# Graph attention and product-key attention: a fourth set of rows fetched one by one, and a reordered start

## The chip, the cores and the metric

The kernel runs on one core of one Trainium2 chip. The metric is the device time of one execution in microseconds (us); before the change it is 10136.64 us, the median of 3 runs (10135.63 to 10138.01).

## The reference

Input: `x` of 8 batches of 1024 tokens of 128 numbers, an adjacency matrix of 1024 x 1024, small weights, and two tables of 131072 rows of 128 numbers (keys and values). Two blocks are added to `x` in turn:

```
x = x + elu(softmax(leaky(e_src + e_dst), masked by adj) @ Wh)      # h = layernorm(x), Wh = h @ W
h = layernorm(x)
q = (h @ Wq) * 128**-0.5                                            # 8 heads of 128
for each of 2 halves: scores against 128 keys, the 16 best          # product keys
of the 16*16 sums the 16 best -> softmax weights kv_scores, table rows ind
k = sum of 16 weighted rows of keys_table[ind];  v = the same of values_table[ind]
out = causal softmax(q k^T) @ v, 1024 x 1024 in each head and batch
x = x + out @ Wo
```

So for each batch, head and token 16 rows of a table must be fetched whose numbers are known only at run time: 8 x 8 x 1024 x 16 rows. Keys and values stand side by side in one table here, so a row is 256 numbers, 1 KB.

## The kernel before

The work is cut into 64 heads (8 batches of 8 heads; n counts them from 0) of 8 units of 128 tokens; (n, t) is unit t of head n. All engines run programs written out by hand and meet only at semaphores.

**VectorE (DVE)** in step t of head n: it chooses the 16 rows of unit (n+1, t) (`choose_sets`, `choose_sums`, `choose_rows`) and, between these, adds up the rows of unit (n, t) that were fetched a head earlier (`add_row`, `sum_rows`, L920 and L931). `choose_rows` leaves the row numbers in `idx` (`idx_ready`, L1006), `sum_rows` frees the buffers (`rows_summed`, L931). So the row numbers of a unit are known about 8 steps before its sum.

**GpSimd (POOL)** fetches: `gathers(t)` (L346) issues one indirect DMA for each of the 16 places of a unit's list, and each brings 128 rows, one for every token, into `ring`, which has room for 4 units. Before unit t of head n it waits for `idx_ready` of that unit and for `rows_summed` of the unit four earlier.

**Single transfers.** For the units in `SETS`, the 16th place is not fetched by POOL but row by row, 128 transfers of 1 KB, into `far`. SyncE (SP) does the sets `FAR = (3, 7)`: `far_begin` copies the 128 addresses into one row of memory (L278), `far_fetch` loads them into registers 32 at a time and issues one transfer each (L293). ScalarE (ACT) does the set of unit 0 (`NEAR`): `near_begin` in step 1 (L468), and `near_fetch` at the end of steps 1 to 7 with 20, 20, 20, 20, 16, 16 and 16 rows (L483). A set may be fetched again only after `rows_summed` of its unit in the head before. Head 0 uses none: POOL issues 128 gathers for it and 125 for each of the 63 others.

**TensorE (PE)** adds the first 8 of 16 rows of a unit as products with diagonal matrices (`weigh`, L656), which ACT makes (`diagonals`, L437), and does all attention products; ACT does the exponentials (`attend_exp`, L446) and copies.

**SP's order.** In each head the sets in turn; at a batch's start `load(b + 2)` (waits until the graph part of the batch before is done, `g_xn`), and in `turn` the eight stores of the finished batch between the two sets.

**The start.** SP issues x, weights, the whole adjacency (4 MB), then the key tensors. PE and ACT make `wh` (own terms, L595), then `dst` (L599), then four groups of key products (L733), then exp, transposes and sum of graph tile 0. DVE makes the mask of all 8 tiles, then the edges of tile 0 (`graph_edges`, L849 to L862). A loop over the 8 tiles of batch 0 follows: finish tile `it` (`graph_elu`, from L872, `graph_out`, `graph_norm`), edges of tile it+1, choose the rows of unit (0, it). From `it = 2` (`LEAD`) on it also sums unit it-2. So units 0 to 5 of head 0 are summed in this loop, and units 6 and 7 (`SUMMED` and the next) only in steps 6 and 7 of head 0.

Of the kernel before, what the change touches and what calls it, by code (L numbers as in the profile page):

```python
# [5 lines left out]
ALU = mybir.AluOpType  # L6
# [8 lines left out]
P = 128  # L15
BATCH = 8
# [16 lines left out]
FAR = (3, 7)  # L33
NEAR = 0
NEAR_ROWS = (0, 20, 20, 20, 20, 16, 16, 16)
SETS = FAR + (NEAR,)
FAR_ROW = TOPK - 1
# [9 lines left out]
def gat_and_product_key_attention(nc, x, adj, W, WT, a, WqpkT, keysT, Wq, table, Wo, out):  # L47
    with ExitStack() as ctx:
# [6 lines left out]
        def sem(name):  # L55
            return ctx.enter_context(nc.semaphore(name))
# [89 lines left out]
        in_dma = sem("in_dma")  # L146
        adj_dma = sem("adj_dma")
# [98 lines left out]
        def _(sp):  # L246
# [33 lines left out]
            def far_fetch(n, i):  # L280

                sp.wait_ge(far_row_dma[i], n * 16)
                sp.sem_inc(sp_mark, 1)
                if not (isinstance(n, int) and n == 1):
                    sp.wait_ge(rows_summed, (n - 1) * UNITS + SETS[i] + 1)
                    sp.sem_inc(sp_mark, 1)
                for q in range(0, P, LOADED):
                    _, at = nc.values_load_multi_w_load_instructions(
                        far_row[0:1, i, q:q + LOADED], engines=[mybir.EngineType.SP],
                        min_val=0, max_val=(HEADS * NUM_KV - 1) * KV_BYTES,  # L290
                        skip_runtime_bounds_check_because="made of two positions below 128 and a head below 8")
                    for j in range(LOADED):
                        sp.dma_start(far[q + j:q + j + 1, i, :].bitcast(U8), table_bytes[bass.ds(at[j], KV_BYTES)]) \  # L293
                            .then_inc(far_dma[i], 16)
# [11 lines left out]
            def turn(b):  # L306
                far_sets((b + 1) * HEADS, range(0, last_set))
                stores(b)
                far_sets((b + 1) * HEADS, range(last_set, last_set + 1))
# [3 lines left out]
            far_begin(1, 0)  # L313
            far_fetch(1, last_set + 1)
            with sp.Fori(1, HEADS) as h:
                far_sets(h, range(len(FAR)))
            with sp.Fori(0, BATCH - 2) as b:
                load(b + 2)
                turn(b)
                with sp.Fori(1, HEADS) as h:  # L320
                    far_sets((b + 1) * HEADS + h, range(len(FAR)))
            turn(BATCH - 2)
            with sp.Fori(1, HEADS - 1) as h:
                far_sets((BATCH - 1) * HEADS + h, range(len(FAR)))
            far_sets(BATCH * HEADS - 1, range(len(FAR)), True)
# [41 lines left out]
        def _(act):  # L367
            def projection(bn):
# [5 lines left out]
                for t in range(TILES):  # L374
                    act.wait_ge(wh_mm, TILES * bn + t + 1)
                    nc.scalar.copy(wh[:, t, :], ps_p[:, t % 2, 0:P + 1]).then_inc(wh_copied, 1)
                for c in range(2):
                    act.wait_ge(dst_mm, 2 * bn + c + 1)
                    nc.scalar.copy(dst[:, c * 512:(c + 1) * 512], ps_p[:, c, :]).then_inc(dst_copied, 1)

# [89 lines left out]
            def near_fetch(n, part):  # L470

                if NEAR_ROWS[part - 1] == 0:
                    act.wait_ge(far_row_dma[near], n * 16)
                    act.sem_inc(act_mark, 1)
                    act.wait_ge(rows_summed, (n - 1) * UNITS + NEAR + 1)
                    act.sem_inc(act_mark, 1)
                q = sum(NEAR_ROWS[:part])
                _, at = nc.values_load_multi_w_load_instructions(
                    far_row[0:1, near, q:q + NEAR_ROWS[part]], engines=[mybir.EngineType.Activation],
                    min_val=0, max_val=(HEADS * NUM_KV - 1) * KV_BYTES,  # L480
                    skip_runtime_bounds_check_because="made of two positions below 128 and a head below 8")
                for j in range(NEAR_ROWS[part]):
                    act.dma_start(far[q + j:q + j + 1, near, :].bitcast(U8), table_bytes[bass.ds(at[j], KV_BYTES)]) \  # L483
                        .then_inc(far_dma[near], 16)
# [4 lines left out]
            projection(0)  # L489

            for g in range(4):
                act.wait_ge(pk_mm, g + 1)
                nc.scalar.copy(pk[:].rearrange("p h s n -> p (h s n)")[:, g * 512:(g + 1) * 512],
                               ps_s[:, g % 2 * 512:(g % 2 + 1) * 512]).then_inc(pk_copied, 1)
            act.wait_ge(in_dma, 4 * 16)
# [19 lines left out]
            def head(b, h, n, graph, ahead, first=False):  # L515
                if ahead and not first:
                    query_weights((h + 1) % HEADS, n + 1)
                for t in range(UNITS):
# [21 lines left out]
                    if t < UNITS - 1:  # L540
                        if not first or t + 1 > SUMMED:
                            diagonals(n, t + 1)
                    elif ahead:
                        diagonals(n + 1, 0)
# [8 lines left out]
                    if ahead and t >= 1 and not first:  # L553
                        near_fetch(n + 1, t)
# [20 lines left out]
        def _(pe):  # L575
            def projection(bn):
# [14 lines left out]
                for t in range(TILES):  # L591

                    if t >= 2:
                        pe.wait_ge(wh_copied, TILES * bn + t - 1)
                    nc.tensor.matmul(ps_p[:, t % 2, 0:P + 1], hnT[:, t * P:(t + 1) * P], w_ext[:],  # L595
                                     start=True, stop=True).then_inc(wh_mm, 1)
                pe.wait_ge(wh_copied, TILES * (bn + 1))
                for c in range(2):
                    nc.tensor.matmul(ps_p[:, c, :], w_dst[:], hnT[:, c * 512:(c + 1) * 512],  # L599
                                     start=True, stop=True).then_inc(dst_mm, 1)  # L600

# [123 lines left out]
            projection(0)  # L725

            pe.wait_ge(in_dma, 4 * 16)
            for g in range(4):
                if g >= 2:
                    pe.wait_ge(pk_copied, g - 1)  # L730
                for j in range(4):
                    m = 4 * g + j
                    ins = nc.tensor.matmul(ps_s[:, (4 * (g % 2) + j) * P:(4 * (g % 2) + j + 1) * P],  # L733
                                           wpk_t[:, m, :], keys_t[:, m, :], start=True, stop=True)
                ins.then_inc(pk_mm, 1)
            pe.wait_ge(dst_copied, 2)
            graph_transposes(0)
            graph_sum(0, 0, ps_s)
# [12 lines left out]
            def head(b, h, n, graph, ahead, first=False):  # L751
# [52 lines left out]
        def _(dve):  # L804
# [217 lines left out]
            projection(0)  # L1022
            dve.wait_ge(adj_dma, 16)
            for t in range(TILES):
                c = step(nc.vector.tensor_scalar(mask[:, t, :], mask[:, t, :].bitcast(I32), 0, -BIG,
                                                 ALU.is_le, ALU.mult))
            after(c)
            graph_edges(0, 0, 0)
            for it in range(TILES):
                graph_elu(it, it, ps_s)  # L1030
# [12 lines left out]
                choose_rows(it, it, c)  # L1043
                weights(it, it)
# [18 lines left out]
            def head(b, h, n, graph, ahead, first=False):  # L1063
                for t in range(UNITS):
# [16 lines left out]
                    dve.wait_ge(dve_rows_dma[t], gathered(n, t))  # L1081
                    if first and t < SUMMED:
# [69 lines left out]
```

## Time and profile before

| | before |
|---|---|
| time, median of 3 runs | 10136.64 us |
| span of the profiled execution | 10159.7 us |
| POOL busy | 7625.7 us (75%), 8003 gathers |
| DVE busy | 6962.0 us (69%) |
| PE busy | 5615.2 us (55%) |
| ACT busy | 3117.0 us (31%) |
| single transfers of SP, of ACT | 16256, 7936 |

The profile gives one execution; its own time is known only as the span, which is 23.1 us over the median of the runs. Busy time leaves out the time that an engine takes to issue DMAs, so ACT's 31% holds none of its 7936 single transfers, and SP has no busy time at all. For POOL the gather itself counts, and the short stretch between two gathers is shown as "issue".

### The profile page before, as it was taken

The page shows a single profiled execution, that of the slowest core. Times are in us where ns is not written, and L with a number is a line of the kernel's source. Part 1 is how long each engine was busy: PE and PEld are TensorE (multiplying, and loading weights), DVE is VectorE, ACT ScalarE, POOL GpSimd, SP SyncE. Part 2 cuts the span into 40 slices and gives each one's busy share as a digit, 9 for nine tenths or more (in the row PEclk, how much of TensorE's full clock was granted, in tenths as well). Part 3 has the DMA queues.
Part 4 walks back from the last instruction along what each step waited for, and adds up shares of the span by engine and source line. Part 5 has one row for each costly group of instructions (what it writes and reads, how often), then busy time and mean ns, then how long its engine had stood idle before and what let it go on. Part 6 is the DMA issues. An engine that isn't in the chain of part 4 may idle for free.

```text
span 10159.7 us, 173542 instructions
## 1 busy us (share of the span) xinstructions
PE 5615.2 (55%) x23108; PEld 4511.4 (44%) x23108; DVE 6962.0 (69%) x42780; ACT 3117.0 (31%) x9770; POOL 7625.7 (75%) x8020
## 2 busy tenths in 40 slices
PE   5655555555555555555555555555555555555555
PEld 4544444444444444444444444444444444444444
DVE  8866667666666667666776666766667676666663
ACT  4333233332333333333333233333333333322222
POOL 5777777777777777777777777777777777777776
PEclk7777777777777777777777777777777777777777
DMA  3333333333333333333333333333333333333333
GB/s 109 104 108 108 108 112 108 108 108 108 112 108 107 108 108 112 108 108 108 108 112 108 108 108 108 112 108 108 107 110 110 108 108 108 108 110 108 108 108 99
DMA packets 481297, 1099.25 MB, mean 108 GB/s; under 512 B 180864, under 2 KB 222720, under 8 KB 479968
## 3 DMA queue, kind: packets, MB, share of 16 engines
q0 software_dynamic: 384144, 1049.48, 36.1%
q1 hardware_dynamic: 71152, 31.60, 1.2%
q10 hardware_dynamic: 24800, 8.19, 0.4%
q14 instruction: 1184, 9.70, 0.3%
q8 instruction: 17, 0.28, 0.0%
HBM read 1084.36 MB, written 4.19 MB: 107 GB/s over the span
## 4 chain that ended last, share of the span: by engine, by line
POOL 73%; issue 24%; DVE 2%; PE 1%; POOLq 0%; DMA 0%; ACT 0%; ACTq 0%; SPq 0%; DVEq 0%
POOL ring L346 73%; DVE hot L998 0%; PE ps_o L709 0%; DMA wo<-in_Wo 0%; DVE ps_v L920 0%; POOLq L362 0%; PE ps_p L595 0%; POOLq L360 0%; DMA ring<-in_table,idx 0%; PE ps_p L599 0%; ACTq L483 0%; PE ps_s L681 0%; DVE nmax L1049 0%; PE ps_w L656 0%; DVE edge L849 0%
## 5 line engine op out<-in xcount | busy, mean ns | idle before, releaser
L346 POOL DMA_INDIRECT ring<-in_table,idx x8003 | 7624.1, 953 | 2507.7 <-issue 2440.8
L656 PE MATMUL ps_w<-ring,diag 128*128 128x256 f32 x8192 | 1996.2, 400 | 9.7 <-DMA ring<-in_table,idx 9.6
L700 PE MATMUL ps_p<-ident,prob 128*128 128x128 f32 x2304 | 548.8, 390 | 2576.1 <-ACT prob L446 2568.1
L656 PEld LDWEIGHTS ps_w<-ring,diag 128*128 128x128 f32 x8192 | 1630.3, 205 | 244.8 <-issue 12.7
L917 DVE TENSOR_SCALAR ps_v<-ring,wgt 128x256 f32<-128x256 f32 x512 | 248.7, 486 | 2147.8 <-DMA ring<-in_table,idx 2147.8
L998 DVE SCALAR_TENSOR_TENSOR hot<-rank,posf,cand 128x54 f32<-128x54 f32 x8192 | 1655.4, 270 | 0.3
L700 PEld LDWEIGHTS ps_p<-ident,prob 128*128 128x128 f32 x2304 | 371.4, 194 | 2769.7 <-ACT prob L446 1734.0
L920 DVE SCALAR_TENSOR_TENSOR ps_v<-ring,wgt,ps_v 128x256 f32<-128x256 f32 x3072 | 1478.1, 481 | 19.6
L437 ACT ACTIVATE diag<-ident,wgt 128x128 f32<-128x128 f32 x4096 | 1251.9, 391 | 0.0
L668 PE MATMUL ps_t<-ident,kv 128*128 128x128 f32 x512 | 234.4, 458 | 1642.4 <-DVE kv L931 1642.4
L709 PEld LDWEIGHTS ps_o<-probT,kv 128*128 128x128 f32 x4608 | 1040.8, 318 | 145.9 <-ACT probT L454 69.9
L446 ACT ACTIVATE prob<-ps_s,nmax 128x128 f32<-128x128 f32 (+7 forms) x512 | 378.1, 738 | 2324.8 <-issue 1777.3
L709 PE MATMUL ps_o<-probT,kv 128*128 128x128 f32 x4608 | 1035.4, 404 | 43.7 <-ACT probT L454 43.7
L668 PEld LDWEIGHTS ps_t<-ident,kv 128*128 128x128 f32 x512 | 92.1, 180 | 1803.4 <-DVE kv L931 1802.7
L681 PE MATMUL ps_s<-kT,qT 128*128 128x512 f32 (+3 forms) x1536 | 784.6, 630 | 1.6 <-issue 1.2
L998 DVE DVE_READ_ACCUMULATOR hot<-rank,posf,cand 128x1 f32 x8192 | 651.3, 79 | 0.0
L634 PE MATMUL ps_v<-pk,xt 128*128 (+1 forms) x1026 | 545.6, 632 | 13.6 <-ACT xt L412 7.5
L931 DVE TENSOR_TENSOR kv<-part,ps_w 128x256 f32<-128x256 f32 x512 | 215.7, 421 | 453.9 <-PE ps_o L709 407.0
L454 ACT COPY probT<-ps_p 128x512 f32<-128x512 f32 (+3 forms) x768 | 351.7, 480 | 414.2 <-PE ps_p L700 412.3
L681 PEld LDWEIGHTS ps_s<-kT,qT 128*128 128x128 f32 x1536 | 366.7, 271 | 194.9 <-issue 188.2
L441 ACT COPY kT<-ps_t 128x128 f32<-128x128 f32 x512 | 135.9, 265 | 977.6 <-PE ps_t L668 977.4
L941 DVE MAX8 side<-ps_v 128x8 f32<-128x128 f32 x1024 | 253.6, 289 | 212.2 <-issue 181.0
(119 smaller groups left out, 8053.9 us busy)
## 6 DMA issues: line engine op xcount, KB each, us to landing
far<-in_table SPq DMA_DIRECT2D x16256, 1.0 KB
ring<-in_table,idx POOLq DMA_INDIRECT x8003
far<-in_table ACTq DMA_DIRECT2D x7936, 1.0 KB
xin<-in_x SPq DMA_DIRECT2D x8, 512.0 KB, 4.6
mask<-in_adj SPq DMA_DIRECT2D x1, 4096.0 KB, 14.6
out_x<-acc SPq DMA_DIRECT2D x64, 64.0 KB
far_row<-far_at SPq DMA_DIRECT2D x127, 0.5 KB
far_row<-far_at ACTq DMA_DIRECT2D x62, 0.5 KB
```

The costliest lines, as they stand in the source:

```text
L346: pool.indirect_dma_start(out=ring[:, t % RING, k, :], out_offset=None, in_=table, in_offset=bass.IndirectOffsetOnAxis(ap=idx[:, t, k:k + ...
L437: nc.scalar.mul(diag[:, k, :], ident[:], wgt[:, t, k:k + 1]).then_inc(diag_ready, 1)
L446: nc.scalar.activation(prob[:, 0:cols], ps_s[:, 0:cols], ACT.Exp, bias=nmax[:, 0:1], accum_out=psum_row[:, 0:1]).then_inc(p_exp, 1)
L454: nc.scalar.copy(probT[:, c * 512:c * 512 + m], ps_p[:, c, 0:m]).then_inc(p_copied, 1)
L634: nc.tensor.matmul(ps_sim, xt[:, t % 2, :], pk[:, bass.ds(h, 1), :, :].rearrange("p o s n -> p (o s n)"), start=True, stop=True).then_inc( ...
L656: ins = nc.tensor.matmul(pw_ps, diag[:, k, :], ring[:, t % RING, k, :], start=(k == 0), stop=(k == PE_ROWS - 1))
L668: nc.tensor.transpose(ps_t[:, 0, :], kv[:, t, 0:P], ident[:]).then_inc(k_tp, 1)
L681: nc.tensor.matmul(ps_s[:, c * 512:c * 512 + m], q, kT[:, c * 512:c * 512 + m], start=True, stop=(c < HALVES[t] - 1))
L700: ins = nc.tensor.transpose(ps_p[:, c, (j % 4) * P:(j % 4 + 1) * P], prob[:, j * P:(j + 1) * P], ident[:])
L709: ins = nc.tensor.matmul(oT_ps, kv[:, j, P:KV], probT[:, j * P:(j + 1) * P], start=(j == 0), stop=(j == t))
L920: row_sum[0] = step(nc.vector.scalar_tensor_tensor(out=part[:] if k == TOPK - 1 else ps_part, in0=rows, scalar=w, in1=ps_part, op0=ALU.mul ...
L998: c = step(nc.vector.scalar_tensor_tensor(out=hot[:, k, :], in0=rank[:], scalar=posf[:, k:k + 1], in1=cand[:, 1, :], op0=ALU.is_equal, op1 ...
```

## The change

- `FAR = (1, 3, 6)` instead of `(3, 7)`; with unit 0 there are four sets, so POOL has 124 gathers in each head from head 1 on.
- SP fetches rows 32 to 127 of unit 1's set and all rows of the sets of units 3 and 6: 352 in a head, 256 before.
- ACT fetches the set of unit 0 in steps 1 to 5 (28, 28, 24, 24, 24 rows) and rows 0 to 31 of unit 1's set in steps 6 and 7 (16 each), the latter in head 0 too: 160 in a head, 128 before.
- SP begins the next set (`far_begin`) before the last 32 rows of the one it is in, not before its first; the batch's stores move to the same place in the third set.
- Start: the adjacency's first tile is loaded ahead of the keys and the rest behind them; `dst` is made before the own terms; graph tile 0's exp, transposes and sum (now in `wh_ps`) move ahead of the last two groups of key products; the masks of tiles 1 to 7 move behind the edges of tile 0; the edges of tile 1 move behind the choice of unit (0, 0).
- Head 0: units 6 and 7 are weighed and summed in steps 1 and 2 (`LATE`), and in these two steps PE waits for the sum before the next similarities.

```diff
-FAR = (3, 7)
+LATE = {1: SUMMED, 2: SUMMED + 1}
+FAR = (1, 3, 6)
 NEAR = 0
-NEAR_ROWS = (0, 20, 20, 20, 20, 16, 16, 16)
+SHARED = 0
 SETS = FAR + (NEAR,)
+ACT_ROWS = (32, 0, 0, P)
+NEAR_PLAN = {1: ((3, 0, 28),), 2: ((3, 28, 56),), 3: ((3, 56, 80),), 4: ((3, 80, 104),), 5: ((3, 104, 128),),
+             6: ((0, 0, 16),), 7: ((0, 16, 32),)}
...
-            sp.dma_start(mask[:].bitcast(I32), adj.rearrange("(t p) n -> p t n", p=P)).then_inc(adj_dma, 16)
-            sp.dma_start(wpk_t, WqpkT).then_inc(in_dma, 16)
-            sp.dma_start(keys_t, keysT).then_inc(in_dma, 16)
+            sp.dma_start(mask[:, 0, :].bitcast(I32), adj[0:P, :]).then_inc(adj_first_dma, 16)
+            sp.dma_start(wpk_t, WqpkT).then_inc(pk_dma, 16)
+            sp.dma_start(keys_t, keysT).then_inc(pk_dma, 16)
+            sp.dma_start(mask[:, 1:TILES, :].bitcast(I32), adj[P:N, :].rearrange("(t p) n -> p t n", p=P)) \
+                .then_inc(adj_dma, 16)
...
-                for q in range(0, P, LOADED):
+                for q in range(first, P, LOADED):
+                    if q == P - LOADED:
+                        if follow is not None:
+                            far_begin(*follow)
+                        if after_begin is not None:
+                            stores(after_begin)
...
-            def far_sets(n, sets, final=False):
-                for i in sets:
+            def far_sets(n, final=False, stored=None):
+                for i in range(len(FAR)):
                     if i < last_set:
-                        far_begin(n, i + 1)
-                    elif not final:
-                        far_begin(n + 1, 0)
-                    far_fetch(n, i)
+                        far_fetch(n, i, ACT_ROWS[i], follow=(n, i + 1))
+                    else:
+                        far_fetch(n, i, ACT_ROWS[i], stored, None if final else (n + 1, 0))
...
             with sp.Fori(0, BATCH - 2) as b:
                 load(b + 2)
-                turn(b)
+                far_sets((b + 1) * HEADS, stored=b)
...
+            projection(0, True)
+            graph_exp(0)
+            keep_products(range(2))
+            graph_copy(0)
+            keep_products(range(2, 4))
+            act.wait_ge(in_dma, 2 * 16)
             nc.scalar.copy(wq_cur[:], wq[:, 0, :]).then_inc(wq_copied, 1)
-            graph_exp(0)
-            graph_copy(0)
...
-                    if ahead and t >= 1 and not first:
-                        near_fetch(n + 1, t)
+                    if ahead:
+                        for i, lo, hi in NEAR_PLAN.get(t, ()):
+                            if i == SHARED or not first:
+                                near_fetch(n + 1, i, lo, hi)
...
+            pe.wait_ge(pk_dma, 2 * 16)
+            key_products(range(2))
+            pe.wait_ge(wh_copied, TILES)
             graph_transposes(0)
-            graph_sum(0, 0, ps_s)
+            graph_sum(0, 0, wh_ps)
+            key_products(range(2, 4))
+            pe.wait_ge(in_dma, 2 * 16)
...
-                    if not first or t >= SUMMED:
+                    if not first:
                         weigh(n, t, graph)
+                    elif t in LATE:
+                        weigh(n, LATE[t], False)
...
+                        if first and t in LATE:
+                            pe.wait_ge(rows_summed, LATE[t] + 1)
                         similarities(n1 % HEADS, n1 * UNITS + t1, t1)
...
-                if it < TILES - 1:
+                if 0 < it < TILES - 1:
                     graph_edges(0, it + 1, it + 1)
                 c = choose_sets(0, it, it)
...
                 choose_rows(it, it, c)
+                if it == 0:
+                    graph_edges(0, 1, 1)
                 weights(it, it)
...
+                    u = LATE.get(t, t) if first else t
+                    dve.wait_ge(dve_rows_dma[u], gathered(n, u))
+                    if first and u != t:
+                        c = choose_sums(n, u, a_unit, c, add_row)
+                        sum_rows(n, u)
+                        choose_rows(t, a_unit, c)
```

## Rows read from the trace of the kernel before

**Rows 1.** The page, part 4: the chain that ended last, by engine
```profile
POOL 73%; issue 24%; DVE 2%; PE 1%; POOLq 0%; DMA 0%; ACT 0%; ACTq 0%; SPq 0%; DVEq 0%
```

**Rows 2.** Waits of POOL: us in total, times, longest us
```profile
POOL ring L346 <- DVE idx L1006: 55.8, 1, 55.8
POOL ring L346 <- DVE kv L931: 11.1, 4, 10.2
```

**Rows 3.** Windows, gathers alone: stretch, length, busy (count), clock, DMA share, GB/s
```profile
58.00:308.90 250.90, 183.09 (x190) 0.77 0.36 103
...
308.90:10135.00 9826.10, 7441.03 (x7813) 0.73 0.38 109
```

**Rows 4.** Timeline of POOL: start us, us, instruction, idle before and releaser
```profile
58.08 1.10 POOL L346 DMA_INDIRECT ring<-in_table,idx  x1 [55.80 <-DVE idx L1006]
...
78.52 1.14 POOL L346 DMA_INDIRECT ring<-in_table,idx  x1 [0.30 <-issue]
...
308.93 0.95 POOL L346 DMA_INDIRECT ring<-in_table,idx  x1 [0.30 <-issue]
...
10133.13 0.94 POOL L346 DMA_INDIRECT ring<-in_table,idx  x1 [0.30 <-issue]
```

**Rows 5.** Timeline of SP, one set in head 7
```profile
1262.81 0.49 SPq L278 DMA_DIRECT2D far_row<-far_at  x1
1265.76 48.38 SPq L293 DMA_DIRECT2D far<-in_table  x128
```

**Rows 6.** Waits of SP, whole span
```profile
SPq L276 <- DVE idx L1006: 3170.9, 126, 32.4
```

**Rows 7.** Timeline of ACT, one part of the set of unit 0
```profile
1110.71 6.65 ACTq L483 DMA_DIRECT2D far<-in_table  x20
```

**Rows 8.** Waits of DVE, 1100 to 1257 us, one head
```profile
DVE ps_v L917 <- DMA ring<-in_table,idx: 37.1, 7, 7.8
```

**Rows 9.** Timeline of DVE and POOL: sum of unit (16, 0), first gather of (16, 4)
```profile
2636.19 0.42 DVE L931 TENSOR_TENSOR kv<-part,ps_w 128x256 f32<-128x256 f32 x1 [8.99 <-PE ps_o L709]
...
2667.61 0.95 POOL L346 DMA_INDIRECT ring<-in_table,idx  x1 [0.30 <-issue]
```

**Rows 10.** Timeline of all engines, the start
```profile
12.77 4.70 PE L595 MATMUL ps_p<-w_ext,hnT 128*128 128x129 f32 x16 [0.68 <-ACT hnT L373]
...
17.82 3.78 PE L599 MATMUL ps_p<-hnT,w_dst 128*128 128x512 f32 x4 [0.36 <-ACT wh L376]
...
22.40 1.67 DVE L849 SCALAR_TENSOR_TENSOR edge<-dst,wh,mask 128x256 f32<-128x256 f32 x4
...
24.98 6.96 PE L733 MATMUL ps_s<-ring 64*128 64x128 f32 x32 [3.37 <-DMA wo<-in_Wo]
...
34.07 1.15 ACT L383 ACTIVATE hn<-edge,row 128x1024 f32<-128x1024 f32 x1
...
42.03 0.35 DVE L872 TENSOR_SCALAR hp<-ps_s,row 128x128 f32<-128x128 f32 x1 [6.52 <-PE ps_s L617]
...
42.67 0.31 ACT L393 ACTIVATE hneg<-hneg 128x128 f32<-128x128 f32 x1 [4.65 <-DVE hneg L874]
...
44.99 1.67 DVE L849 SCALAR_TENSOR_TENSOR edge<-dst,wh,mask 128x256 f32<-128x256 f32 x4
...
46.31 1.22 PE L634 MATMUL ps_v<-pk,xt 128*128 128x256 f32 x2 [0.85 <-ACT xt L412]
...
49.55 0.49 DVE L941 MAX8 side<-ps_v 128x8 f32<-128x128 f32 x2
...
57.63 0.17 DVE L1006 CAST idx<-idxf 128x16 uint32<-128x16 f32 x1
...
74.00 0.17 DVE L1006 CAST idx<-idxf 128x16 uint32<-128x16 f32 x1
```

**Rows 11.** Timeline of ACT and DVE, end of head 0 and sum of unit (1, 0)
```profile
291.07 1.11 ACT L446 ACTIVATE prob<-ps_s,nmax 128x1024 f32<-128x1024 f32 x1 [3.22 <-DVE nmax L1049]
...
296.45 0.42 DVE L931 TENSOR_TENSOR kv<-part,ps_w 128x256 f32<-128x256 f32 x1 [0.70 <-PE ps_o L709]
```

More of the change, by code:

```diff
@@ L367, in _, with own_terms, projection @@
         def _(act):
-            def projection(bn):
+            def own_terms(bn):
+                for t in range(TILES):
+                    act.wait_ge(wh_mm, TILES * bn + t + 1)
+                    nc.scalar.copy(wh[:, t, :], ps_p[:, t % 2, 0:P + 1]).then_inc(wh_copied, 1)
+            def projection(bn, dst_first=False):
                 act.wait_ge(hvar, bn + 1)
@@ L373, in projection @@
                     nc.scalar.copy(hnT[:, c * 512:(c + 1) * 512], ps_p[:, c, :]).then_inc(hnT_copied, 1)
-                for t in range(TILES):
-                    act.wait_ge(wh_mm, TILES * bn + t + 1)
-                    nc.scalar.copy(wh[:, t, :], ps_p[:, t % 2, 0:P + 1]).then_inc(wh_copied, 1)
+                if not dst_first:
+                    own_terms(bn)
                 for c in range(2):
@@ L488, in _, with keep_products @@
             nc.scalar.copy(w_dst[:], wh_ps[:, 1:P + 1]).then_inc(aux_copied, 1)
[L489 to L495, printed above, removed]
+            def keep_products(groups):
+                for g in groups:
+                    act.wait_ge(pk_mm, g + 1)
+                    nc.scalar.copy(pk[:].rearrange("p h s n -> p (h s n)")[:, g * 512:(g + 1) * 512],
+                                   ps_s[:, g % 2 * 512:(g % 2 + 1) * 512]).then_inc(pk_copied, 1)
+            projection(0, True)
[4 more added lines that the diff above has]
+            act.wait_ge(in_dma, 2 * 16)
             nc.scalar.copy(wq_cur[:], wq[:, 0, :]).then_inc(wq_copied, 1)
-            graph_exp(0)
-            graph_copy(0)
             for it in range(TILES):
@@ L539, in head @@
                     attend_begin(n, t)
[L540 to L543, printed above, removed]
+                    if first and t == 1:
+                        diagonals(n, SUMMED + 1)
+                    if not first and t < UNITS - 1:
+                        diagonals(n, t + 1)
+                    elif ahead and t == UNITS - 1:
                         diagonals(n + 1, 0)
@@ L575, in _, with own_terms, projection @@
         def _(pe):
-            def projection(bn):
+            def own_terms(bn):
+                for t in range(TILES):
+                    if t >= 2:
+                        pe.wait_ge(wh_copied, TILES * bn + t - 1)
+                    nc.tensor.matmul(ps_p[:, t % 2, 0:P + 1], hnT[:, t * P:(t + 1) * P], w_ext[:],
+                                     start=True, stop=True).then_inc(wh_mm, 1)
+            def projection(bn, dst_first=False):
                 if not isinstance(bn, int):
@@ L590, in projection @@
                     pe.wait_ge(aux_copied, 2)
[L591 to L597, printed above, removed]
+                if not dst_first:
+                    own_terms(bn)
+                    pe.wait_ge(wh_copied, TILES * (bn + 1))
                 for c in range(2):
@@ L724, in _, with key_products @@
             pe.wait_ge(consts, 5 + HEADS)
[L725 to L736, printed above, removed]
+            projection(0, True)
+            def key_products(groups):
+                for g in groups:
+                    if g >= 2:
+                        pe.wait_ge(pk_copied, g - 1)
+                    for j in range(4):
+                        m = 4 * g + j
+                        ins = nc.tensor.matmul(ps_s[:, (4 * (g % 2) + j) * P:(4 * (g % 2) + j + 1) * P],
+                                               wpk_t[:, m, :], keys_t[:, m, :], start=True, stop=True)
+                    ins.then_inc(pk_mm, 1)
+            pe.wait_ge(pk_dma, 2 * 16)
+            key_products(range(2))
+            pe.wait_ge(wh_copied, TILES)
             graph_transposes(0)
-            graph_sum(0, 0, ps_s)
+            graph_sum(0, 0, wh_ps)
+            key_products(range(2, 4))
+            pe.wait_ge(in_dma, 2 * 16)
             for it in range(TILES):
@@ L1022, in _, with masks @@
             projection(0)
-            dve.wait_ge(adj_dma, 16)
[L1024 to L1028, printed above, removed]
+            def masks(tiles):
+                for t in tiles:
+                    c = step(nc.vector.tensor_scalar(mask[:, t, :], mask[:, t, :].bitcast(I32), 0, -BIG,
+                                                     ALU.is_le, ALU.mult))
+                after(c)
+            dve.wait_ge(adj_first_dma, 16)
+            masks(range(1))
+            dve.wait_ge(wh_copied, 1)
+            graph_edges(0, 0, 0)
+            dve.wait_ge(adj_dma, 16)
+            masks(range(1, TILES))
+            dve.wait_ge(wh_copied, TILES)
             for it in range(TILES):
-                graph_elu(it, it, ps_s)
+                graph_elu(it, it, ps_s if it else wh_ps)
                 graph_out(0, it, it, True)
                 graph_norm(it)
-                if it < TILES - 1:
+                if 0 < it < TILES - 1:
                     graph_edges(0, it + 1, it + 1)
```

49 lines of the change are left out of this document (25 added, 24 removed).

## The prediction

> **What bounds the kernel now.** I read the page first and in it the chain of waits: POOL and the "issue" between its gathers make 97% of the chain that ended last [rows 1]. The waits of POOL say whether it is ever held up: 55.8 us before its first gather, and 11.1 us in 4 waits for a sum of DVE, 10.2 of them in one [rows 2]; going through all 8003 gathers in the timeline, that one, at 259 to 269 us, is the only place where a gather starts over 1.6 us after the one before. The busy shares mislead here: POOL is shown 75% busy and is never free. The windows give the pace. From the 191st gather at 308.93 to the end of the last, which starts at 10133.13, there are 7813 [rows 3, 4]; (10133.13 + 1.25 - 308.93) / 7813 = 1.2576 us each. So the time is the start of the first gather, 8003 gathers at 1.26 us, one wait, and a tail of 10159.7 - 10134.4 = 25.3 us after the last.
>
> The sum below is made against the profiled execution, whose span is 10159.7 us, 23.1 us (0.23%) over the median 10136.64. I take the saving off both alike.
>
> **One gather less in each of 63 heads.** Head 1 has 61 gathers in its first four units instead of 62, and 62 more are saved behind them. I count the 62 here: 62 x 1.2576 = 78.0 us. The one of head 1 comes up below. It is worth this only if the 128 rows are fetched beside POOL in time, so each cover is checked.
>
> **SP.** A set of 128 rows takes 48.38 us, 0.378 us a row, and 2.95 us pass from the copy of the addresses to the first row [rows 5]. 352 rows are 133.1 us; the three begins are issued inside the sets now, so their landing is mostly hidden: 4 us a head is my estimate, 9 the upper bound (three times 2.95). SP needs 137 to 142 us of a head of 124 x 1.2576 = 155.9 us. It fits with 14 to 19 us to spare; before it waited 3170.9 us for row numbers [rows 6], some 50 us a head. At each batch's start `load` now stands ahead of the set of unit 1 and waits for the graph's tile of step 5, which holds that set back by some 4 steps (80 us). The sets have about 8 steps (156 us) from row numbers to sum, and SP makes up 14 us or more in each head: cost nothing, at most a few us if a set is late. The stores stand behind a wait for the row numbers of step 1, by when DVE has added the last unit of the batch: nothing.
>
> **ACT.** 20 rows take 6.65 us, 0.333 us each [rows 7]; 32 more rows are 10.7 us a head: 8 more rows (2.7 us) in steps 1, 2 and 5, 4 more (1.3 us) in steps 3 and 4. Queued behind them is the next `attend_exp`, for which PE waits, then `turn_keys` and similarities, then DVE. So I let all of it fall on DVE's loop. The cover is that DVE stands idle 37.1 us of a head for rows of POOL [rows 8]; 26 us remain. POOL feels DVE's lateness only through the ring. It is tightest at the batches' starts, where PE and ACT make the projection: the sum of unit (16, 0) ends at 2636.6 and the gather that needs it starts at 2667.6, a margin of 31 us [rows 9]. A head's 10.7 us and the 1.3 us by which POOL comes earlier leave 19. Cost nothing; without the cover it would be up to 12 us in each of 6 batches. DVE's extra address column is one small instruction a head, under the same cover.
>
> **The start, up to the first gather.** `dst` takes from its first product to the edges 22.40 - 17.82 = 4.6 us; made first, it is ready at 12.77 + 4.6 = 17.4. The first own term adds 1, so the edges of tile 0 begin at 18.4 and, as the block takes 49.55 - 44.99 = 4.6, end at 23.0 [rows 10]. ACT has the own terms until 22.4, then loads the exp's table (1.3) and starts the exp at 23.7, against 34.07 [rows 10]. From that start to the tile's sum read by DVE it was 42.03 - 34.07 = 8.0; half the key products, 3.5 us of 6.96, keep PE until 25.7, which adds 0.7: 32.3. But ACT now has to copy the last two key groups, which PE makes from 32.3 to 35.8, before the tile's next exponential: that runs at 36.5, not at 33. From there to the end of the similarities it was 46.31 + 1.22 - 42.67 = 4.9: 41.4. Choosing takes 57.80 - 49.55 = 8.25: row numbers at 49.6, first gather at 49.9, 8.2 us earlier than 58.08.
>
> **The second unit takes that back.** POOL is through with unit (0, 0) 20.4 us later, at 70.3 [rows 4]. The edges of tile 1 now start only when unit 0 is chosen: 49.6 + 4.6 = 54.2, exp, transposes and sum 8.0: 62.2, and from there to row numbers 57.80 - 42.03 = 15.8: 78.0, against 74.17 before [rows 10]. So POOL starts unit (0, 1) at 78.3, against 78.52: it waits 8 us and has won 0.2. Bounds: 70.3 (no wait, 8.2 won) and 82 (3.5 lost). I take the worked-out value. DVE is 3.8 us late in the rest of the loop, and POOL, with the list 4.3 us ahead there before, still does not wait.
>
> **Head 0.** Summing units 6 and 7 in steps 1 and 2 takes away what POOL waited 10.2 us for. What is late next is the sum of unit (1, 0), which frees the ring for (1, 4). It ended at 296.9 [rows 11]. It comes later by the loop's 3.5 us (0.3 made good) and by ACT's 32 rows in steps 6 and 7, 10.7 us of which its idle time before the exponentials covers 3.2 [rows 11] and, I estimate, 1.5 in the step before: 6 us. The two sums only change places. That gives 306.4. POOL, held by nothing, would be there at 308.93 - 10.2 - 1.3 (head 1's gather less) - 0.2 = 297.2. It waits 9 us, and (1, 4) starts at 306.6: 2.3 us won. Bounds for this place: 297 less a few us if DVE runs earlier too (up to 12 won) and 316 (ACT's rows and PE's two new waits for the sum all on the path, 7 lost). Units (1, 5) to (2, 3) follow with margins of 3 to 10 us by the same reckoning; the tail stays.
>
> **Sum.** 78.0 + 2.3 = 80.3 us: span 10079.4, time 10136.6 - 80.3 = 10056.3, say 10056. Its own range is 10047 to 10066, from the bounds of the last paragraph.
>
> **Rivals.** (a) Both early gains last: unit (0, 1) does not wait and (1, 4) does not: 78.0 + 10.2 + 1.3 + 8.2 = 97.7, 10039. For it: the start is indeed shorter; against it: the dependence through the edges of tile 1. (b) POOL meets new waits later, at batches' starts or while DVE catches up in heads 1 to 3: 1 to 4 us in each of 7 places, 10060 to 10084. For it: ACT's rows fall where DVE catches up, and in head 1 SP has all its sets to do at once; against it: the 31 us margin. (c) Slower: SP becomes the bound. It decides from 352 r + 4 = 157.2 (the head before), r = 0.435 us a row; each 0.01 beyond costs 3.5 us a head, 222 us in all, so r = 0.45 gives about 10460. Against it: 0.378 was measured with ACT issuing at the same time. (d) The row-by-row transfers slow the gathers as much as they replace them, and nothing is won: 10137. Against it: the DMA engines are busy 38% of the time [rows 3], and POOL's pace is set by issuing, not by landing.
>
> The Trainium skill speaks for (d): in "DMA: Bandwidth & Descriptors", section "Issuing engines are not separate DMA queues", it says that DMAs started by different engines run on the same 16 DMA engines, and that spreading them saves only the sequencer's issue time. If the DMA engines were the bound, this change would bring nothing. Here the issue time is exactly what binds, so rule and forecast agree on this trace, and the rule would bite only with the DMA share near full.
>
> **How the numbers follow.** Forecast 66%, (a) 10%, (b) 18%, (c) 3%, (d) 3%. The range 10042 to 10074 holds the forecast, half of (a) and most of (b). It also takes in that the gathers' pace may move: 0.001 us each is 8 us in all, and DVE's work per gather rises by 0.8%. 0.2% is about what a measurement of this kernel can tell from none, 20 us. Faster by more than that are the forecast, (a) and (b): 0.94. Same 0.03 (d), slower 0.03 (c).
>
> **What would show it.** Right: 7940 gathers at 1.257 to 1.259 us; the first near 50, the second unit's first near 78 with a wait of about 8 us on row numbers; no wait near 259; one of several us for a sum near 297; none after 320; SP's sets at 48.4 us for 128 rows, with its wait for row numbers down to some 15 us a head. Wrong: waits of POOL in every head or batch, rows of SP above 0.40 us, a pace off 1.2576 by more than 0.002, or a first gather later than 58.

## The result, and the profile after

The changed kernel takes 10064.62 us (median of 4 runs, 10059.83 to 10070.11) beside 10137.33 us for the kernel before: ratio 0.9927, 95% interval 0.9915 to 0.9939. It saves 72.7 us; 80 were forecast.

| | before | after |
|---|---|---|
| time, median | 10137.33 us | 10064.62 us |
| span of the profiled execution | 10159.7 us | 10063.9 us |
| gathers | 8003 | 7940 |
| POOL, DVE, ACT busy | 7625.7, 6962.0, 3117.0 us | 7545.1, 6958.9, 3072.9 us |

The two spans differ by 95.8 us, the times by 72.7, because the profile of before comes from an execution 23 us slower than its median: its gathers follow each other at 1.2576 us, those of after at 1.2549 us, which over 7813 gathers makes 20.9 us that the change did not bring. Below, "pace" is this time from one gather's start to the next where POOL never waits.

Waits of POOL in the kernel after (us in total, times, longest) answer to [rows 2]; the waits are now one of idx before the first gather and one before the second unit, and a long one filed under "issue":

```profile
POOL ring L352 <- issue: 2438.8, 7933, 19.5
POOL ring L352 <- DVE idx L1040: 54.8, 6, 45.7
```

Timeline of POOL after, beside [rows 4]; start, duration, and in brackets the idle time before:

```profile
47.96 1.10 POOL L352 DMA_INDIRECT ring<-in_table,idx  x1 [45.68 <-DVE idx L1040]
...
67.10 0.97 POOL L352 DMA_INDIRECT ring<-in_table,idx  x1 [0.30 <-issue]
76.01 0.94 POOL L352 DMA_INDIRECT ring<-in_table,idx  x1 [7.95 <-DVE idx L1040]
...
292.86 0.95 POOL L352 DMA_INDIRECT ring<-in_table,idx  x1 [0.30 <-issue]
313.33 0.99 POOL L352 DMA_INDIRECT ring<-in_table,idx  x1 [19.52 <-issue]
...
10038.83 0.95 POOL L352 DMA_INDIRECT ring<-in_table,idx  x1 [0.30 <-issue]
```

The gather at 313.33 is the first of unit (1,4), the same place as 308.93 in [rows 4]. The profile names no releaser, but the sum it needs, of unit (1,0), ends just ahead of it. Timeline of DVE after, the sums of units (0,5), (1,0) and (2,0):

```profile
186.84 0.42 DVE L965 TENSOR_TENSOR kv<-part,ps_w 128x256 f32<-128x256 f32 x1
...
312.11 0.42 DVE L965 TENSOR_TENSOR kv<-part,ps_w 128x256 f32<-128x256 f32 x1 [8.27 <-PE ps_o L734]
...
456.32 0.42 DVE L965 TENSOR_TENSOR kv<-part,ps_w 128x256 f32<-128x256 f32 x1 [9.81 <-PE ps_o L734]
```

The windows view of the gathers from there on (columns as in [rows 3]):

```profile
313.20:10041.00 9727.80, 7362.62 (x7751) 0.74 0.39 110
```

Nothing waits in this stretch. So in the two traces: 62 gathers less, 77.8 us at 1.2549; (1,4) starts 4.4 us later; the tail is 1.5 us shorter; 20.9 us are pace. 77.8 - 4.4 + 1.5 = 74.9, against 72.7 by the times.

### The profile page after: what moved, and what is told of

Same layout as the page of the kernel before. It is cut to its first block, busy times and chain, and to the rows that moved or that the text cites. A ratio compares the mean times of both kernels' runs of the same rounds, so it can differ in the third digit from the quotient of the medians.

```text
span 10063.9 us, 190428 instructions
## 1 busy us (share of the span) xinstructions
PE 5503.5 (55%) x23108; PEld 4468.0 (44%) x23108; DVE 6958.9 (69%) x42844; ACT 3072.9 (31%) x9770; POOL 7545.1 (75%) x7957
## 4 chain that ended last, share of the span: by engine, by line
POOL 72%; issue 24%; DVE 2%; PE 1%; ACTq 1%; POOLq 0%; ACT 0%; DMA 0%; SPq 0%; DVEq 0%
POOL ring L352 72%; ACTq L495 1%; DVE hot L1032 0%; PE ps_o L734 0%; DVE ps_v L954 0%; DVE edge L883 0%; POOLq L368 0%; PE ps_s L706 0%; PE ps_p L725 0%; DVE edge L896 0%; POOLq L366 0%; DVE row L887 0%; ACT L409 0%; ACTq L490 0%; PE ps_v L659 0%
## 5 line engine op out<-in xcount | busy, mean ns | idle before, releaser
L352 POOL DMA_INDIRECT ring<-in_table,idx x7940 | 7543.5, 950 | 2494.0 <-issue 2438.8
L725 PE MATMUL ps_p<-ident,prob 128*128 128x128 f32 x2304 | 589.3, 413 | 3391.8 <-ACT prob L458 3391.6
L725 PEld LDWEIGHTS ps_p<-ident,prob 128*128 128x128 f32 x2304 | 402.6, 207 | 3586.1 <-ACT prob L458 2374.9
L734 PEld LDWEIGHTS ps_o<-probT,kv 128*128 128x128 f32 x4608 | 1013.9, 311 | 150.2 <-ACT probT L466 84.2
L706 PE MATMUL ps_s<-kT,qT 128*128 128x512 f32 (+3 forms) x1536 | 751.3, 607 | 1.6 <-issue 1.2
L659 PE MATMUL ps_v<-pk,xt 128*128 (+1 forms) x1026 | 528.7, 615 | 19.1 <-DVE kv L965 11.4
L1092 DVE TENSOR_REDUCE nmax<-ps_s 128x1 f32<-128x128 f32 (+7 forms) x512 | 382.7, 747 | 0.0
```

The costliest lines, as they stand in the source:

```text
L352: pool.indirect_dma_start(out=ring[:, t % RING, k, :], out_offset=None, in_=table, in_offset=bass.IndirectOffsetOnAxis(ap=idx[:, t, k:k + ...
L659: nc.tensor.matmul(ps_sim, xt[:, t % 2, :], pk[:, bass.ds(h, 1), :, :].rearrange("p o s n -> p (o s n)"), start=True, stop=True).then_inc( ...
L706: nc.tensor.matmul(ps_s[:, c * 512:c * 512 + m], q, kT[:, c * 512:c * 512 + m], start=True, stop=(c < HALVES[t] - 1))
L725: ins = nc.tensor.transpose(ps_p[:, c, (j % 4) * P:(j % 4 + 1) * P], prob[:, j * P:(j + 1) * P], ident[:])
L734: ins = nc.tensor.matmul(oT_ps, kv[:, j, P:KV], probT[:, j * P:(j + 1) * P], start=(j == 0), stop=(j == t))
L1092: nc.vector.tensor_reduce(nmax[:], ps_s[:, 0:(t + 1) * P], AX_X, ALU.max, negate=True) \
```

## The experiments

POOL is the bound from unit (1,4) on, so where that unit starts is what each kernel did at the start. This number is sharper than the time, since the pace of the gathers wanders by 0.002 us (20 us in all) between executions of one kernel. All starts are from each kernel's POOL timeline. A second profile of the changed kernel has (1,4) at 311.7 instead of 313.3, so differences of under 2 us in this table mean nothing. "Sum (1,0)" is the end of its L931 or the same line there.

| kernel | unit (0,1) starts | sum (1,0) ends | unit (1,4) starts | ratio to before, 95% |
|---|---|---|---|---|
| before | 78.5 | 296.9 | 308.9 | |
| after | 76.0 | 312.5 | 313.3 | 0.9927 (0.9915 to 0.9939) |
| sets only | 77.9 | 307.3 | 309.7 | 0.9925 (0.9912 to 0.9939) |
| start only | 76.6 | 300.6 | 301.4 | 0.9987 (0.9978 to 0.9996) |
| SP alone in head 0 | 76.5 | 297.7 | 298.5 | 0.9919 (0.9905 to 0.9932) |
| few large transfers | 74.5 | 296.4 | 297.2 | 0.9901 (0.9885 to 0.9916) |
| old start, early sums | 77.3 | 310.1 | 310.9 | 0.9926 (0.9910 to 0.9941) |
| edges of tile 1 early | 70.8 | 303.3 | 304.1 | 0.9917 (0.9902 to 0.9933) |
| three sets in head 1 | 74.6 | 296.2 | 297.0 | 0.9912 (0.9899 to 0.9926) |
| both of these | 70.1 | 288.6 | 289.7 | 0.9904 (0.9889 to 0.9919) |

**Which part brings what.** The sets alone: the start and head 0 as in the kernel before (`projection(0)`, one load of the adjacency, all key products first, `weigh` and the sums at `t >= SUMMED`).

> The four sets and the new order on SP, but the old start and units 6 and 7 of head 0 summed in steps 6 and 7 as before. Theory (the 63 gathers are all of the gain, and the sum of unit (1,0) sets where POOL stands after the start): POOL's first gather at 58, a wait of about 10 us before unit (1,2), then unit (1,4) starts between 309 and 316, as in the changed kernel (313.3); the time is that of the changed kernel, within 5 us of 10065. Rival (the new start is worth what the earlier first gather shows, 10 us, and the removed wait another 10): 10075 to 10085.

Measured: 10087.20 us beside 10162.73 (most executions on that chip had the slower pace, of both kernels), 75.5 us saved. The 10087 is near the rival's 10075 to 10085 and 22 us over the theory's 10065, but the kernel before is 25 us slower there too, so the times do not decide between them; where the units start does, and it is as the theory had it. One wait, of 13.1 us, before unit (1,2), then (1,4) at 309.7: all of the saving is the 63 gathers, and the rest of the change adds nothing to it that the times show.

The start alone, with three sets (`FAR = (3, 7)` and the old orders of SP and ACT):

> The new start and the early sums of units 6 and 7, with the old three sets (125 gathers a head). Theory (ACT's 32 single transfers in steps 6 and 7 of head 0 are what made the sum of unit (1,0) late, 312.5 against 296.9): without them that sum ends at 295 to 299, unit (1,4) starts at 296 to 299, and about 11 us are saved against the kernel before: 10126. Rival 1 (the moved sums and PE's new wait for them made it late): unit (1,4) starts at 308 or later, 10137. Rival 2 (the early first gather counts in full): 10117 or less.

Measured: 10150.08 us beside 10162.73; the one run of each at the quicker pace, 10128.29 beside 10135.51. Unit (1,4) starts 7.6 us earlier. The sum of (1,0) ends at 300.6: 3.7 us later than before where the theory had none, 11.9 earlier than in the changed kernel. Of the 3.7 us, 2.2 are a wait for SP's rows, which this kernel has because with the old order SP starts on unit (1,0)'s rows only when unit (1,3) is chosen. Waits of DVE from 290 to 302 us:

```profile
DVE part L951 <- DMA far<-in_table: 2.2, 1, 2.2
```

Three kernels below that have the early sums and the new start but none of ACT's rows in head 0 (SP alone, few large transfers, three sets in head 1) end this sum at 296.2 to 297.7, as early as the kernel before (296.9). So the early sums and the new start cost it nothing by themselves, and the 15.6 us by which it is later after the change come with ACT's 32 rows. Without the early sums and with the old start (the sets alone) the same rows cost 10.4 us.

The old start with sets and early sums:

> The changed kernel with the old start (sets and early sums kept). Theory (the end of the start's loop is the same, 187.3 us in both traces, so the new start is worth nothing at unit (1,4)): first gather at 58, no wait at unit (0,1), a wait of about 19 us before (1,4), which starts at 312 to 315: the changed kernel's time within 3 us. Rival (the earlier start is worth 2 to 8 us): (1,4) at 316 or later.

Measured: 10062.72 us (10061.91 to 10063.25). First gather at 56.8, no wait at the second unit, (1,4) at 310.9, even 2.4 us before the changed kernel's. The first gather 9 us earlier is worth nothing in the change as it was made.

**ACT's rows in head 0.**

In head 1's sets SP begins at row 0 of unit (1,1) (`whole`):

```diff
-                            if i == SHARED or not first:
+                            if not first:
...
-            with sp.Fori(1, HEADS) as h:
+            far_sets(1, whole=True)
+            with sp.Fori(2, HEADS) as h:
```

> The changed kernel, but in head 0 SP fetches all 128 rows of unit (1,1)'s set and ACT none; later heads as changed. Theory (ACT's rows in head 0): the sum of unit (1,0) ends near 298, POOL's wait of 19 us before unit (1,4) shrinks to 5 or less, 14 to 18 us are saved against the changed kernel: about 10049. SP is 12 us later through head 1, which may cost a few us there. Rival (PE's wait for the early sums): the wait stays near 19 us, 10065.

Measured: 10055.62 us in the run at the quicker pace (10135.51 before), 10078.92 to 10081.87 in the others. Unit (1,4) starts at 298.5, 14.8 us earlier than after the change, as the theory had it, but a new wait stands behind it. The POOL timeline and, below, the waits of DVE between 340 and 370 us of this kernel:

```profile
364.74 0.99 POOL L353 DMA_INDIRECT ring<-in_table,idx  x1 [7.34 <-issue]
```

```profile
DVE part L955 <- DMA far<-in_table: 20.9, 1, 20.9
```

SP, with 32 rows more to do, is late with the set of unit (1,3), and POOL pays 7 us for it at (1,7). In all 9 us are left of the 14 to 18 expected. In the changed kernel ACT holds back the attention. Its timeline there, at the end of steps 6 and 7 of head 0, shows each part of the set and the exponential queued behind it:

```profile
280.99 7.40 ACTq L495 DMA_DIRECT2D far<-in_table  x16
288.43 1.01 ACT L458 ACTIVATE prob<-ps_s,nmax 128x896 f32<-128x896 f32 x1 [8.85 <-issue]
...
298.65 5.00 ACTq L495 DMA_DIRECT2D far<-in_table  x16
...
304.24 1.11 ACT L458 ACTIVATE prob<-ps_s,nmax 128x1024 f32<-128x1024 f32 x1
```

In [rows 11] the same exponential ran at 291.07 after 3.2 us of idle time: 13 us earlier. With SP alone in head 0 it runs at nearly the same time, and ACT is idle before it about as long:

```profile
291.88 1.11 ACT L459 ACTIVATE prob<-ps_s,nmax 128x1024 f32<-128x1024 f32 x1 [2.74 <-DVE nmax L1093]
```

The timeline leaves out one instruction. Before each part ACT loads the part's addresses from `far_row` into registers, and this is time on ACT too. The source view of that line, 270 to 310 us (count, then shortest, median and longest in ns):

```profile
L490 ACTq TENSOR_LOAD <-far_row x2: 1198/1209/1220, 279.4 to 297.4; - x2
```

So the two parts hold ACT for 1.2 + 7.8 and 1.2 + 5.1 us, 15.3 in all. The first is longer because the very first of ACT's row transfers takes 2.5 us instead of 0.22.

**Neither engine has the rows in head 1.** POOL makes that gather itself, for unit (1,1) alone:

```diff
+            for t in range(UNITS):
+                pool.wait_ge(idx_ready, UNITS + t + 1)
+                pool.wait_ge(rows_summed, UNITS + t - RING + 1)
+                gathers(t, t == SETS[0])
-            with pool.Fori(1, BATCH * HEADS) as n:
+            with pool.Fori(2, BATCH * HEADS) as n:
```

> The changed kernel, but in head 1 unit (1,1) has no set: POOL makes that gather itself (7941 in all), ACT has no single transfers in head 0, SP three sets in head 1. Theory (ACT's rows in head 0 held the sum of unit (1,0) for 11 us; with them on SP, SP was late for unit (1,3)): (1,4) starts at 299 to 302 and there is no wait at (1,7): 11 to 14 us less one gather of 1.3, so 10 to 13 us saved against the changed kernel. Rival (another wait takes the place of each that goes): 5 us or less.

Measured: 10048.50 us (10046.99 to 10050.37), 16.1 less than the changed kernel and 3 more saved than the upper end of what I expected. (1,4) at 297.0, no wait behind it.

**The second unit.** `if it < TILES - 1: graph_edges(0, it + 1, it + 1)` ahead of `choose_sets` for tile 0 too:

> The changed kernel, but the edges of tile 1 stand ahead of the choice of unit (0,0) as before. Theory (the wait of 8.9 us before the second unit comes from the moved edges): first gather 2 us later, near 50, no wait at unit (0,1), which starts near 71 instead of 76; the loop's end comes 3 to 5 us earlier, and so does (1,4): 308 to 310 instead of 313.3, 4 us saved. Rival (the wait has another cause, or DVE is the bound of the loop): the wait stays, or the loop's end does not move, and the time is that of the changed kernel.

Measured: 10054.97 us (10050.70 to 10058.03). First gather at 50.3, 2.3 us later than in the changed kernel, and the second unit right behind it at 70.8, with no wait in POOL's list:

```profile
POOL ring L352 <- DVE idx L1040: 48.0, 1, 48.0
```

The loop's last sum, of (0,5), ends at 178.9 instead of 187.3, and (1,4) starts 9.3 us earlier; I had expected 3 to 5.

Both together:

> The two edits together: no set for unit (1,1) in head 1, and the edges of tile 1 ahead of the choice of unit (0,0). Theory: both add up, unit (1,4) at 294 to 297, 16 us saved against the changed kernel, 89 to 92 us against the kernel before. Rival: the sum of unit (1,0) does not follow the start, 12 us.

Measured: 10040.91 us (10040.70 to 10041.43) beside 10137.50, ratio 0.9904 (0.9889 to 0.9919): 96.6 us under the kernel before and 23.7 under the changed one. POOL has no wait after its first gather:

```profile
POOL ring L355 <- issue: 2421.2, 7939, 0.3
POOL ring L355 <- DVE idx L1047: 47.6, 2, 47.3
```

The same kernel without the early sums:

> The best kernel so far with units 6 and 7 of head 0 summed in steps 6 and 7 as in the kernel before. Theory (the early sums are worth their wait once nothing else holds unit (1,4)): POOL waits 11 to 14 us before unit (1,2), 11 to 13 us more in all: 10052 to 10054. Rival (as in the kernel with the sets alone, where unit (1,4) started at 309.7 against 310.9 with early sums, they are worth nothing): 10041.

Measured: 10052.06 us (10050.11 to 10055.22), 11.1 us more; POOL waits once, before (1,2):

```profile
260.80 0.94 POOL L355 DMA_INDIRECT ring<-in_table,idx  x1 [11.80 <-DVE kv L967]
```

So the early sums are worth 11 us once nothing else holds (1,4), and nothing in the change as it was made.

**Does POOL's pace suffer from single transfers?** The kernel with few large ones leaves out the fetch by row number, so its sums are of other rows:

```diff
-                    for j in range(LOADED):
-                        sp.dma_start(far[q + j:q + j + 1, i, :].bitcast(U8), table_bytes[bass.ds(at[j], KV_BYTES)]) \
+                        sp.dma_start(far[rows, i, :], table[rows, :]).then_inc(far_dma[i], 16)
```

> The changed kernel with each part of a set as one transfer of rows known beforehand (4 or 5 transfers of 16 to 32 rows a set instead of 128 of one row): the rows summed are the wrong ones, everything else is computed. It takes away all issue time of single transfers on SP and ACT and their small packets. Theory (POOL's pace is set by its own issuing): the pace of the gathers stays at 1.2550 us within 0.001; only POOL's wait before unit (1,4) shrinks, as ACT is free in head 0: 10047 to 10052. Rival (the single transfers take from the gathers, as all run on the same DMA engines): the pace falls by 0.005 us or more, 10020 or less.

Measured: 10061.60 us (10059.40 to 10063.01). (1,4) starts at 297.2, and from there 7751 gathers take

```profile
297.20:10034.30 9737.10, 7373.67 (x7751) 0.74 0.38 109
```

which is 1.2562 us each, 0.0012 over the theory's 1.2550 and so just outside its 0.001, but inside the 1.2549 to 1.2573 that the changed kernel itself shows in two profiles. (1,4) starts at 297.2; the time is 10 us over its forecast, which is pace again: 7751 x 0.0013. Taking the single transfers away did not quicken the gathers, and with three sets a head (start only) and with four (both of these) the pace is the same 1.2546. Rival (d) falls: an effect of single transfers on the gathers, if there is one, is smaller than the 0.0024 by which the pace moves by itself. The same kernel gives the price of ACT's rows: from the sum of (1,0) to that of (2,0), where the loop of DVE, PE and ACT catches up and never waits for POOL, it takes 115.6 us (296.4 to 412.05), against 144.2 after (312.5 to 456.7) and 135.3 before (296.9 to 432.2), where 9.0 of the 135.3 are waits for SP's rows. So ACT's 160 rows cost the loop 28.6 us, while they hold ACT for 63.7 us of a head, address loads included: a good half is covered.

The changed kernel once more, with the next three:

> The changed kernel itself once more, on the chip and beside the runs of the three others, since the pace of the gathers differs a little from execution to execution. Expected: 10060 to 10070, 72 to 76 us under the kernel before.

Measured: 10067.15 us (10061.60 to 10084.44); the profiled execution has a span of 10082.6, with (1,4) at 311.7 and a pace of 1.2573: 18.7 us over the first profile, all of it pace.

**How much room is left.** On the best kernel, SP takes ACT's 32 rows (`ACT_ROWS = (0, 0, 0, P)`):

> The best kernel so far (three sets in head 1, edges of tile 1 early), but SP fetches all of unit (.,1)'s set: 384 rows a head, ACT 128. Reckoned from the trace of the changed kernel SP needs 384 x 0.378 + 3 x 3.3 = 155 us of a head of 155.6. Theory (rows cost 0.378 us whatever the load, and the sets have some 80 us to spare): SP never waits for row numbers but keeps up, the time stays within 5 us of 10041. Rival (SP at its limit falls behind at each batch's start, where load holds it back by 80 us, and does not make it good): POOL waits in later batches, 30 us or more.

Measured: 10211.25 us (10208.81 to 10214.91), ratio 1.0071 (1.0055 to 1.0088), slower than the kernel before. Waits of SP, then of DVE, over the whole span:

```profile
SPq L284 <- DVE idx L1046: 28.5, 2, 28.4
```

```profile
DVE part L960 <- DMA far<-in_table: 1639.3, 162, 32.6
```

SP, which waited 3170.9 us for row numbers in [rows 6] and 230.2 us in the changed kernel, hardly waits for them any more, and DVE waits for SP's rows instead. The sets still take 48.5 us each, but a head now takes SP 158 us (first begin to first begin, most heads), not the 155 that I had reckoned, and POOL needs 155.6. So SP is not only late at the batches' starts, it loses 2 to 3 us in every head, until POOL waits, first at 2736 us. The theory is wrong; the rival is right that POOL waits, by 170 us instead of its 30 or more, and tells only part of the cause.

ACT takes 64 rows more, SP 64 fewer (`ACT_ROWS = (96, 0, 0, P)`, 48 rows each in steps 6 and 7):

> The best kernel so far, but ACT fetches rows 0 to 95 of unit (.,1)'s set in steps 6 and 7 (48 each): 224 rows a head on ACT, 288 on SP. 64 more rows are 21 us of ACT a head. DVE stands idle for rows 1642.6 / 63 = 26 us a head in the changed kernel. Theory (all of ACT's rows fall on the loop of PE and DVE, POOL feels it only when the loop's lateness passes the 31 us margin of a batch's start): DVE's idle time for rows falls to some 5 us a head, and POOL waits at the batches' starts, 0 to 60 us in all: 10045 to 10100. Rival (ACT's rows run beside PE and DVE and cost the loop little): DVE's idle time falls by less than 10 us a head, no waits of POOL, 10041.

Measured: 10952.08 us (10949.24 to 10959.52), ratio 1.0804 (1.0786 to 1.0822). POOL waits in each of heads 2 to 62, 923 us in all. Timeline of DVE, the sums of unit 0 in two heads that follow each other, then of ACT in steps 6 and 7:

```profile
3384.45 0.42 DVE L972 TENSOR_TENSOR kv<-part,ps_w 128x256 f32<-128x256 f32 x1 [24.37 <-PE ps_o L741]
...
3555.34 0.42 DVE L972 TENSOR_TENSOR kv<-part,ps_w 128x256 f32<-128x256 f32 x1 [24.63 <-PE ps_o L741]
```

```profile
4009.74 17.11 ACTq L502 DMA_DIRECT2D far<-in_table  x48
4027.19 1.01 ACT L465 ACTIVATE prob<-ps_s,nmax 128x896 f32<-128x896 f32 x1 [19.18 <-issue]
...
4037.69 16.90 ACTq L502 DMA_DIRECT2D far<-in_table  x48
```

A head takes 170.9 us. Without waiting for POOL the best kernel takes 142.9 (288.6 to 431.5 in head 1), so 64 rows cost 28.0 us (in head 1 itself, 169.0 against 142.9, 26.1). ACT spends 24.7 us on them, address loads included, so nothing of them is covered any more. Both theory and rival fall: the cover was far smaller than DVE's idle time says.

## Why the prediction was right

**The gathers: right.** 62 at 1.2549 instead of 1.2576 us. The kernel with the sets alone saves 75.5 us by this alone.

**SP: right in the outcome, its cost mis-sized.** I gave SP 137 to 142 us a head, and it takes 145.5. Timeline of SP after, one set and the begin behind it:

```profile
1157.60 0.50 SPq L286 DMA_DIRECT2D far_row<-far_at  x1
1160.65 48.46 SPq L306 DMA_DIRECT2D far<-in_table  x128
1209.32 0.49 SPq L286 DMA_DIRECT2D far_row<-far_at  x1
1212.28 48.68 SPq L306 DMA_DIRECT2D far<-in_table  x128
```

I read the 3 us between a begin and the next row as the landing of the addresses, which the new order would hide. It is not a landing: most of it is again the load of the next 32 addresses into registers, which stands ahead of every 32 rows, begin or no begin, and which the timeline leaves out. The source view of that line:

```profile
L301 SPq TENSOR_LOAD <-far_row x697: 2023/2130/2414, 206.8 to 9927.7; - x175
```

A begin itself costs 0.7 us. The 48.4 us that I took for 128 rows hold only three of their four loads, so "0.378 us a row" is short by one load in each set, and moving the begins could not save it. The loop's jump back, 2.4 us a head, was not counted either. The margin is 10 us, not 14 to 19, and SP waits 230.2 us for row numbers, under 4 us a head, not the 15 that I gave as a sign. The set that `load` holds back at a batch's start costs nothing, as forecast: DVE waits for far rows twice in the whole span, 3.6 us. SP 384 shows what happens when the margin is gone.

**ACT's cover: held, but mis-sized on both sides.** I set 10.7 us of rows against 37.1 us of DVE's idle time for rows [rows 8] and left 26. With its two address loads the 32 rows take ACT 12.9 us (twice 1.20 + 5.24). Catching up, a head takes the loop 144.2 us after the change: of a head of 155.6 us only 11.4 are spare. DVE's idle time for POOL's rows is no such room; PE's wait for ACT's exponential rose from 2568.1 to 3391.6 us in all, and I take it that with the rows there earlier DVE would have waited for PE. The margins of the ring held all the same. The smallest after head 1 is 12.4 us, at (2,4); from head 4 on none is under 29 us, and at (16,4), where I had left 19 of 31 us [rows 9], it is 31.3.

**The first gather and the second unit: right.** 47.96 for 49.9, a wait of 8 us before unit (0,1), which starts at 76.0 for 78.3. "Edges of tile 1 early" shows the cause: with the old place of the edges the wait is gone.

**Head 0: the mechanism right, two terms mis-sized.** The sum of (1,0) was the next thing late, but it ends at 312.5, not 306.4, and (1,4) starts at 313.3, not 306.6. The two misses have opposite signs. The 3.5 us from the loop are not there: (0,5) is summed at 187.3 in both kernels; the shorter start would bring it to 178.9, and the moved edges take all of that back, no more. ACT's rows I let fall on the path with 6 us; they cost 15.6. Of these, 4.6 are rows priced too low: 15.3 us on ACT instead of 10.7, by two address loads and the slow first transfer. The cover was as I took it, 4.7 us by the forecast and 1.7 + 2.7 us of idle time before the two exponentials in the kernel with SP alone. Another 2.5 us arise behind the last exponential: the sum follows it by 8.3 us, and by 5.8 before. What makes these 2.5 us and the rest, about 2, stays open; the sets alone, where the sums still fill these two steps, lose only 10.4 in all. That is 6.7 us for unit (1,4); less the 1.5 of the tail, and with the 0.2 by which 62 gathers at the quicker pace are worth less, it is the difference between 80.3 and 74.9. The forecast came out closer than its terms because one miss took off from the other, and that is luck.

**The rivals.** (b), new waits later, did not come; (c) is real and close, 32 rows away, though by the number of loads and rows and not by a slower row; (d) fell. (a), both early gains kept, is what the best kernel reaches by two edits: 96.6 us against its 97.7.

## What to carry to other kernels

Where one engine's queue sets the pace, count its instructions, and follow every wait of the start until the queue is unbroken: an earlier first instruction is worth nothing if the second waits as long. Size the cover of work added to another engine by the time a stage takes when it catches up, not by the idle time of one of its engines. When a bound is moved from one engine to two others, look at how far each is from its own limit before the next step: here 10 us and 11 us of a head of 156. And take the cost of a part of work from begin to begin: the rows alone left out the address loads, 2 us for every 32 rows on SP.

## What the runs showed of the hardware

The pace of POOL's gathers differs between executions of one kernel, from 1.2549 to 1.2573 us in the two profiles of the changed kernel, and nearly all of it lies in the gathers themselves: their mean duration is 949.9 and 952.1 ns, while the idle time between them is 305 ns in both. The same holds before against after (952.4 and 949.9 ns). In one series 14 of 15 times of the kernel before lay between 10160.68 and 10166.45 us and one at 10135.51; in another all 9 between 10133.27 and 10142.06. What sets it stays open; the kernel without single transfers, at 1.2562, does not stand out.

SP issues a row transfer whose address stands in a register every 0.33 us, whether ACT issues 128, 160 or 224 such transfers a head beside it. Loading the addresses into registers costs 2.13 us for 32 on SP and 1.20, 1.67 and 1.91 us for 16, 24 and 28 on ACT (medians). It is paid again for each group, and the timeline of the profile does not show it. The first row transfer that ACT issues takes 2.5 us in the changed kernel (2.4 to 2.9 in the other four traces with rows in head 0), the next ones 0.22. Why was not tried.
